# Perceiver block on one core: x3 of the pair behind is formed ahead of the first maximum of the pair in front, on VectorE

## The reference, cut to what matters

```python
x = x + xattn(layernorm(x), ctx)          # scores per head, softmax over 128 keys, 16 heads
x = x + attn(layernorm(x))                # softmax(q k^T * scale) v, times Wo, plus bo
x = x + ffn(layernorm(x))                 # below

def ffn(x):
    xh = x @ hadamard
    scale = max(max|xh| over features, 1e-5) / 7
    xq = clip(round(xh / scale), -8, 7) * scale
    return xq @ ternary(weight).T
```

## Time and profile before

| | |
|---|---|
| time, median of 3 runs | 337.03 us (336.73 to 337.52) |
| profiled execution | 338.82 us, of which its span (first to last instruction) 337.0 us |
| TensorE busy | 318.1 us, 94% |
| VectorE busy | 239.7 us, 71% |
| ScalarE busy | 211.1 us, 63% |
| GpSimd busy | 88.2 us, 26% |
| mean granted TensorE clock | 0.992 |

### The profile page before, as it was taken

How to read it: one execution, slowest core, us unless ns; L and a number is a source line. 1 busy time by engine, 2 the same in 40 slices (tenths; PEclk the granted TensorE clock), 3 DMA queues, 4 the chain that set the end, 5 groups by cost and what they waited for, 6 DMA issues and landing times.

```text
span 337.0 us, 8519 instructions
## 1 busy us (share of the span) xinstructions
PE 318.1 (94%) x3204; PEld 231.7 (69%) x3204; DVE 239.7 (71%) x517; ACT 211.1 (63%) x565; POOL 88.2 (26%) x129
## 2 busy tenths in 40 slices
PE   8897899999999999999999999999999999898995
PEld 6775666758595867768585857677685858575754
DVE  1489638686877868686868768686868778686435
ACT  2474858577586758586685867585866757673210
POOL 2000533131332323231223313232312223131320
PEclk9997999999999999999999999999999999999999
DMA  7891203040211303040402103030402020000000
GB/s 227 277 375 59 97 3 124 2 158 0 103 58 38 122 33 124 5 151 0 155 0 94 62 31 124 31 124 5 151 2 65 0 66 0 33 3 31 2 31 31
DMA packets 13481, 25.25 MB, mean 75 GB/s; under 512 B 3216, under 2 KB 3984, under 8 KB 13456
## 3 DMA queue, kind: packets, MB, share of 16 engines
q1 hardware_dynamic: 13456, 24.91, 21.0%
HBM read 20.71 MB, written 4.19 MB: 74 GB/s over the span
## 4 chain that ended last, share of the span: by engine, by line
PE 75%; DVE 15%; DMA 3%; ACT 2%; issue 2%; SPq 2%; DVEq 0%
PE ps L644 17%; PE ps L683 9%; PE ps L600 7%; DVE mx L417 6%; PE ps L768 5%; PE ps L733 5%; PE ps L656 5%; PE ps L687 4%; PE ps L753 4%; DVE x L540 3%; DMA w_rows<-weight 3%; PE ps L615 3%; PE ps L624 2%; PE ps L630 2%; PE ps L649 2%
## 5 line engine op out<-in xcount | busy, mean ns | idle before, releaser
L301 ACT ACTIVATE prob<-ps,nmx,qk_scale 128x128 f32<-128x128 f32 x256 | 95.9, 463 | 56.3 <-DVE nmx L421 56.3
L644 PE MATMUL ps<-had_s,x3t 128*128 128x512 f32 x128 | 59.2, 605 | 1.2 <-ACT x3t L295 1.2
L417 DVE TENSOR_REDUCE mx<-ps 128x8 f32<-128x1024 f32 x32 | 39.0, 1218 | 13.3 <-PE ps L768 13.3
L644 PEld LDWEIGHTS ps<-had_s,x3t 128*128 128x128 f32 x128 | 23.0, 189 | 30.1 <-issue 24.6
L426 DVE TENSOR_REDUCE sum_a<-prob 128x8 f32<-128x1024 f32 x32 | 37.5, 1209 | 2.3 <-ACT prob L301 2.3
L295 ACT ACTIVATE prob_t<-ps 128x512 f32<-128x512 f32 x64 | 35.1, 612 | 5.6 <-PE ps L600 5.5
L600 PE MATMUL ps<-ident,prob 128*128 128x128 f32 x256 | 33.3, 273 | 1.0 <-ACT prob L301 1.0
L288 POOL TENSOR_TENSOR res<-prod,x 128x512 f32<-128x512 f32 x15 | 19.0, 1267 | 57.0 <-DVE prod L530 57.0
L683 PE MATMUL ps<-x2t,wqkv_s 128*128 128x128 f32 x256 | 32.5, 280 | 0.8 <-ACT x2t L295 0.8
L683 PEld LDWEIGHTS ps<-x2t,wqkv_s 128*128 128x128 f32 x256 | 29.8, 191 | 2.0 <-ACT x2t L295 1.2
L284 POOL TENSOR_TENSOR qk_scale<-aux,power 128x1 f32<-128x1 f32 x16 | 8.8, 548 | 83.1 <-DVE aux L496 83.1
(11 more groups left out here) (114 smaller groups left out, 566.0 us busy)
## 6 DMA issues: line engine op xcount, KB each, us to landing
ct<-ctx_cols SPq DMA_DIRECT2D x16, 512.0 KB, 3.7
xt<-x_cols SPq DMA_DIRECT2D x16, 256.0 KB, 2.6
xr<-x_rows SPq DMA_DIRECT2D x16, 256.0 KB, 3.8
y<-res SPq DMA_DIRECT2D x15, 256.0 KB, 2.0
w_rows<-weight SPq DMA_DIRECT2D x1, 1024.0 KB, 10.5
had_s<-hadamard SPq DMA_DIRECT2D x1, 1024.0 KB, 8.6
wqkv_s<-wqkv SPq DMA_DIRECT2D x1, 768.0 KB, 10.2
wqk<-w_qk SPq DMA_DIRECT2D x2, 128.0 KB, 4.1
```

The costliest lines, as they stand in the source:

```text
L301: last = nc.scalar.activation(prob[:, h, :], ps[:, h // 4, (h % 4) * P:(h % 4) * P + P], ACT.Exp, bias=nmx[:, h:h + 1], scale=qk_scale[:])
L417: V.tensor_reduce(mx[:, h], ps[:, 2 * half:2 * half + 2, :].rearrange("p r (c k) -> p (r c) k", c=EC), AX.X, ALU.max).then_inc(done["mx"], 1)
L644: mm = pe.matmul(ps[:, B4, :], x3t[:, c, :], had_s[:, c, :], start=(c == 0), stop=(c == EC - 1))
```

## The change

The last two steps of VectorE's body change places. Before, VectorE waits for the scores of pair i+1, takes the first half's maxima (L417, L421), and then waits for the output projection of pair i-1 and forms x3 (L540). After, it waits for the output projection and forms x3, and then waits for the scores and takes the maxima. Nothing is added or removed, and no other engine's program is touched.

```diff
@@ VectorE's body
                         V.scalar_tensor_tensor(prod[:], ps[:, B4, :], qscale[:], scale_row[:], ALU.mult, ALU.mult)\
                             .then_inc(read["int"], 1)
-                if front:
-                    after(dve, made["s"], i + 1)
-                    largest(i + 1, 0)
                 if self_:
                     after(dve, made["wo"], i - 1)
                     after(dve, done["rsum2"], i - 1)
                     after(dve, done["x2b"], i - 1)
                     after(dve, done["res"], i - 3)
                     V.scalar_tensor_tensor(x3[:, 1 - par], ps[:, B3, :], rsum2[:], x2b[:], ALU.mult, ALU.add)\
                         .then_inc(read["wo"], 1)
+                if front:
+                    after(dve, made["s"], i + 1)
+                    largest(i + 1, 0)
```

## The result

| | before | after |
|---|---|---|
| time, median | 337.27 us (336.73 to 337.85, 4 runs) | 363.63 us (361.98 to 364.30, 4 runs) |
| profiled execution, span | 337.0 us | 360.2 us |
| mean granted TensorE clock | 0.992 | 0.981 |

The account below looks back on a forecast made before the run. The prediction took the stretch from the scores to L644, 3.99 us a pair, as what the change moves. 13 x 1.29 + 1.67 = 18.4 us on 337.0 us gave 355.4 us, range 351.5 to 360.5.

Parts of the forecast that it names:

- What bounds the kernel: A pair costs 3.99 us from the scores to L644 on TensorE, plus 14.59 us behind it without a gap.
- Steps 1 to 4: VectorE to L644: x3 0.38 us earlier, L615's 0.33 us wait shortened, maximum 1.73 us later, copy x3t and L644 held up.
- Step 5, the sum: L644 starts 1.29 us later in 13 bodies, 1.67 us at the step from body 14 to 15: 18.4 us.
- the term for the clock: Rival: TensorE's clock falls in the new 1.6 us gap, 1.7 us each, 363 or 379 us; 8 in 100.
- The shorter wait: Rival: x3 starts before L778's recorded end, or exponentials catch up; L644 0.23 to 1.0 us late, 341 to 351; 6 in 100.
- the copy that isn't held up: Rival: ScalarE's copy x3t doesn't delay L644, which comes 0.38 us earlier a pair, 331.7 us; 2 in 100.
- the delay that is taken up elsewhere: Rival: about 1.3 us of TensorE idle time behind L644 absorbs the delay, time within 0.2%; 1 in 100.
- Behind L644: VectorE's xm, x2, statistics and second maximum come 1.06 us later, less than L644's 1.29 us, so cost nothing on top.

Follow-up runs that it names:

- e3_copy_first: The changed kernel with ScalarE's copy x3t put ahead of all exponentials instead of behind the first four; 349.66 us, ratio 1.035 to the kernel before.
- e5_between: The kernel before with x3 moved between the maximum and nmx on VectorE (maximum, x3, nmx); 339.85 us, ratio 1.005.
- e1_filler: The changed kernel with five idle matmuls on TensorE between L630 and L644 in each pair; 356.22 us, ratio 1.055 to the kernel before.

## Why the prediction was wrong in its number

**What bounds the kernel**: right. What moved the time of the changed kernel went through the distance from the scores to L644. The stretch behind it stayed whole where the clock was whole: from L644's start to the next score group's are 13.35 us in both kernels (163.84 to 177.19, 111.44 to 124.79).

**Steps 1 to 4**: right, each within 0.1 us. The start of x3 (1.17 us behind L778's, 1.16 computed), the 0.67 us to the maximum (0.66), ScalarE's idle time of 4.1 us (4.10) and the gap of 1.6 us (1.61) are in the timeline above. The Trainium skill's rule on the pipe ("VectorE: DVE Perf Modes", section "The DRAIN you can't avoid"), taken to mean 0.75 us, would be 0.09 us off; the row was the better guide. The prediction left out that the same section lets a next operation that is not held back start earlier. The trace agrees with that by its 0.66 us for an operation that needs nothing of x3.

**Step 5, the sum**: right for the queue. From the first score group to the last the kernel with two idle matmuls, free of falls there, takes 304.27 - 45.19 = 259.08 us for 13 bodies and the one before 242.28: 16.8 / 13 = 1.29 us a pair more, against 1.29 computed, and the step to body 15 costs 1.67 against 1.67, 18.5 us together against 18.4.

**What failed is the term for the clock.** The sum has none: it takes the clock in the new gap to stay at 1.00, and the term left at nothing measured 4 x 1.7 = 6.7 us in the profiled execution and 7 to 8 us in the medians. The range of 351.5 to 360.5 allowed for a fall in a few pairs only. The text named it as a rival, "in every pair 14 x 1.7 = 24 us, 379; in a third of them 363", and gave it 8 in 100. The price was right (1.7 us a fall), and so was the place. The one in three was only an example; that it matches the four or five falls of an execution (mean clocks 0.981 and 0.976), and that 363 is the measured time, is luck. I weighed the gap of 1.6 us between two rows, 2.08 us with a fall and 0.77 us without, and let the dense work around the gap decide against it. The 0.77 us was misread as well: it is what the window from 16 to 18 us holds of an idle piece of 1.00 us, which the timeline of the kernel before shows:

```profile
16.77 1.09 PE L600 MATMUL ps<-ident,prob 128*128 128x128 f32 x8 [1.00 <-ACT prob L301]
```

But no row showed an idle stretch of that length in dense work that kept the clock, so there was nothing to decide by; even odds would have been honest, and the range should have reached to about 366. The Trainium skill's remark that a gap can pull the clock down again in every turn of a loop ("TensorE: Matmul & The Clock Gate", section "HAM oscillation — how this bites in real kernels") bears on this case. The trace agrees in part: falls come back around the new gap, but in four pairs of fourteen and not in every turn.

**The other rivals.** The shorter wait, the copy that isn't held up and the delay that is taken up elsewhere didn't occur. The copy ahead of the exponentials was built (e3_copy_first) and would not have given the 331.7 us either: its gain is lost again at L683. That rival was priced without following ScalarE to its next copy.

**Behind L644**: the statement that 1.06 us of lateness costs nothing on top held only because L644 moved by more. Once it doesn't, the second maximum and x2n hold L683 and L649.

What stays open: why the falls come in every third pair in particular and only from the sixth gap on, and where above 1.19 us of idle time they begin to be possible. Gaps of 1.51 us (e5_between) and 1.72 us (e1_filler) at the step to body 15 brought none in the profiled execution.

## What to carry to other kernels

An instruction that starts an engine's next step early is dear when it must itself wait: here 0.38 us for x3 were paid with 1.73 us for the maximum, since VectorE stood waiting for a product while the scores lay ready. Follow what is released late through the other engines' fixed order (nmx, four exponentials, the copy behind them), and over to the next copy as well. A new idle stretch on TensorE has to be priced twice, as waiting and as a possible fall of its clock, and if no row decides the second, the range has to hold both.

## What the runs showed of the hardware that was not expected

TensorE's clock fell to the lower level (1.2 GHz, windows at 0.50) in a kernel whose TensorE is 89% busy. What brought it was an idle stretch of 1.6 to 1.7 us in 19.9 us, though not each time: three of thirteen such gaps had a fall, the sixth, the ninth and the twelfth, and so had the one of 2.84 us at the end, at 1.7 us each. With 1.19 us or less idle in the same place it did not fall in the steady pairs of the profiled executions. One idle matmul of 0.49 us in the gap, which delays nothing, brought 363.6 us down to 357.5.
